# A mixer's numerator summed by an accumulating DMA instead of VectorE, in a two-layer recurrent mixer and mixture-of-experts kernel

## The reference

```python
ek = jnp.exp(jnp.minimum(kf, 30.0))
ekv = ek * vf
# forward and reverse scans over time, a = a * decay + ekv, b = b * decay + ek
euk = jnp.exp(jnp.minimum(u + kf, 30.0))
num = nf + nb - ekv + euk * vf
den = df + db - ek + euk
base = jax.nn.sigmoid(r) * (num / jnp.maximum(den, 1e-08))
out = base * (0.8 + 0.2 * tf)
```

## Time and profile before

| what | value |
|---|---|
| three runs, median (lowest to highest) | 4678.69 us (4672.37 to 4686.97) |
| the profiled execution's span | 4682.9 us |
| TensorE busy in it | 4475.7 us, 96% |
| VectorE busy in it | 2567.2 us, 55% |
| units alone | 0 to about 317 us |
| units beside halves 0 to 5 | about 317 to 1546 us |

### The profile page before, as it was taken

How to read it: one execution, slowest core, us unless ns; L and a number is a source line. 1 busy time by engine, 2 the same in 40 slices (tenths; PEclk the granted TensorE clock), 3 DMA queues, 4 the chain that set the end, 5 groups by cost and what they waited for, 6 DMA issues and landing times.

```text
span 4682.9 us, 60901 instructions
## 1 busy us (share of the span) xinstructions
PE 4475.7 (96%) x19862; PEld 3545.7 (76%) x19863; DVE 2567.2 (55%) x2765; ACT 1789.8 (38%) x2596; POOL 722.8 (15%) x934
## 2 busy tenths in 40 slices
PE   6777999999999999999999999999999999999998
PEld 2245877777777877878888888888888888888887
DVE  8999999999999653433233434444341253333432
ACT  5665555555555333232222323334231142222321
POOL 1000000000000017211111112112111121111111
PEclk8888999999999999999999999999999999999999
DMA  6675767767676766754344545555552254444543
GB/s 226 235 263 184 274 241 268 251 223 282 240 268 226 270 212 190 251 182 111 95 131 112 170 112 160 171 166 150 182 168 57 61 186 145 112 112 116 161 109 61
DMA packets 247928, 835.08 MB, mean 178 GB/s; under 512 B 28160, under 2 KB 61056, under 8 KB 222976
## 3 DMA queue, kind: packets, MB, share of 16 engines
q1 hardware_dynamic: 172944, 572.77, 34.5%
q0 software_dynamic: 47728, 160.07, 15.5%
q10 hardware_dynamic: 27136, 100.67, 5.8%
HBM read 652.40 MB, written 181.01 MB: 178 GB/s over the span
## 4 chain that ended last, share of the span: by engine, by line
PE 80%; DVE 10%; issue 4%; ACT 3%; DMA 2%; POOL 0%; ACTq 0%; DVEq 0%; POOLq 0%; SPq 0%
PE ps L1593 34%; PE ps L1457 22%; PE ps L1607 16%; PE ps L1526 3%; PE ps L1479 1%; PE ps L1582 1%; DVE work L969 1%; DVE work L975 1%; DMA work<-rows_dram,row_idx 1%; PE ps L1477 1%; PE ps L1467 1%; DVE work L996 1%; DVE work L998 1%; DVE work L972 1%; DVE work L1002 1%
## 5 line engine op out<-in xcount | busy, mean ns | idle before, releaser
L1593 PE MATMUL ps<-halves 128*128 128x512 f32 x7152 | 1698.6, 393 | 3.5 <-DVE halves L1356 2.8
L1593 PEld LDWEIGHTS ps<-halves 128*128 128x128 f32 x7152 | 1338.5, 189 | 279.9 <-DVE halves L1356 3.1
L1457 PE MATMUL ps<-halves 128*128 128x512 f32 x6144 | 1450.2, 395 | 13.7 <-issue 12.5
L1457 PEld LDWEIGHTS ps<-halves 128*128 128x128 f32 x6144 | 1154.1, 189 | 287.2 <-issue 47.8
L1607 PE MATMUL ps<-halves 128*128 128x512 f32 x3576 | 834.9, 389 | 1.3 <-DVE halves L1372 1.3
L1607 PEld LDWEIGHTS ps<-halves 128*128 128x128 f32 x3576 | 671.1, 188 | 140.9 <-DVE halves L1372 1.6
L1356 DVE TENSOR_TENSOR halves<-ps,halves 128x1024 fp32r<-128x1024 f32 x150 | 183.7, 1225 | 905.2 <-ACT halves L852 905.2
L1351 DVE TENSOR_TENSOR halves<-work,halves 128x1024 fp32r<-128x1024 f32 (+1 forms) x320 | 440.2, 1433 | 83.6 <-ACT halves L856 83.3
L852 ACT ACTIVATE halves<-ps 128x1024 fp32r<-128x1024 f32 x150 | 154.0, 1027 | 862.4 <-PE ps L1593 862.4
L576 POOL DMA_INDIRECT out<-work,add_idx x149 | 249.8, 1677 | 1417.3 <-DVE work L1378 1382.2
L856 ACT ACTIVATE halves<-work 128x1024 fp32r<-128x1024 f32 (+1 forms) x320 | 369.1, 1229 | 67.0 <-PE ps L1607 56.5
(11 more groups left out here) (186 smaller groups left out, 3674.4 us busy)
## 6 DMA issues: line engine op xcount, KB each, us to landing
halves<-split_dram SPq DMA_DIRECT2D x512, 512.0 KB, 5.6
work<-expert_w SPq DMA_DIRECT2D x192, 1024.0 KB, 5.5
split_dram<-halves ACTq DMA_DIRECT2D x32, 1024.0 KB, 4.9
plain<-shared_w SPq DMA_DIRECT2D x32, 512.0 KB, 3.2
gated_dram<-work ACTq DMA_DIRECT2D x32, 512.0 KB, 4.1
work<-side_t ACTq DMA_DIRECT2D x32, 512.0 KB, 5.6
work<-x_t ACTq DMA_DIRECT2D x32, 512.0 KB, 3.7
ratio_dram<-work ACTq DMA_DIRECT2D x32, 512.0 KB, 4.2
```

The source lines that it names most:

```text
L1457: last = pe.matmul(bank(k % 4), w, op[:, part], start=(c == 0 and w is w_hi and op is hi), stop=(c == CB - 1 and w is w_lo))
L1593: last = pe.matmul(ps_h[:, a * 512:a * 512 + 512], xp[:, xk * P:(xk + 1) * P], wp[:, rhs], start=(xk == 0 and xp is xhi and wp is whi[q]), ...
```

## The change

In the units beside the halves VectorE no longer adds `W` to `G`. GpSimd waits for `W` and for the backward scan, and issues a DMA that reads `W` and adds it to `G` within SBUF. VectorE waits for the DMA's semaphore `num_added` before the last product. In all units the Newton products now work in `F`, so `W` keeps its content, and the wait for `num_w` (or `num`) ahead of the first of them is gone.

```diff
+ALONE = 2 * UNITS_PER_HALF
...
+            def add_numerator(u, l):
+
+                n = u * 2 + l
+                pool.wait_ge(s["wv_done"], n + 1)
+                pool.wait_ge(s["nb"], n + 1)
+                pool.dma_start(G, W, accum_op=ALU.add).then_inc(s["num_added"], 16)
+
             clip(0, 0)
-            with pool.Fori(0, BLOCKS // 2) as v:
+            with pool.Fori(0, ALONE // 2) as v:
                 clip(2 * v + 1, 1)
                 clip(2 * v + 2, 0)
+            for u in range(ALONE, BLOCKS):
+                add_numerator(u, 0)
+                clip(u + 1, (u + 1) % 2)
+                add_numerator(u, 1)
...
                     fill(4 * l + 2)
-                    if not summed_by_pe:
-                        ve.wait_ge(s["nb"], n + 1)
-                        ve.wait_ge(s["wv_done"], n + 1)
-                        ve.tensor_tensor(G, G, W, ALU.add).then_inc(s["num"], 1)
                     fill(4 * l + 3)
-                    if summed_by_pe:
-                        ve.wait_ge(s["num_w"], n + 1)
-                    else:
-                        ve.wait_ge(s["num"], n + 2)
                     ve.wait_ge(s["g_inv"], n + 1)
                     ve.wait_ge(s["den"], n + 1)
-                    ve.scalar_tensor_tensor(W, F, low[:, at], N, ALU.add, ALU.mult).then_inc(s["newton1"], 1)
+                    ve.scalar_tensor_tensor(F, F, low[:, at], N, ALU.add, ALU.mult).then_inc(s["newton1"], 1)
                     ve.wait_ge(s["newton1"], n + 1)
-                    ve.scalar_tensor_tensor(W, W, 2.0, N, ALU.subtract, ALU.mult).then_inc(s["newton2"], 1)
+                    ve.scalar_tensor_tensor(F, F, 2.0, N, ALU.subtract, ALU.mult).then_inc(s["newton2"], 1)
                     ve.wait_ge(s["newton2"], n + 1)
                     if summed_by_pe:
                         ve.wait_ge(s["num"], n + 2)
-                    ve.scalar_tensor_tensor(N, NUM if summed_by_pe else G, neg_gain[:, ds(u, 1)], W, ALU.mult, ALU.mult)\
+                    else:
+                        ve.wait_ge(s["num_added"], 16 * (n - 2 * ALONE + 1))
+                    ve.scalar_tensor_tensor(N, NUM if summed_by_pe else G, neg_gain[:, ds(u, 1)], F, ALU.mult, ALU.mult)\
```

More of the change, by code:

```diff
@@ L205, in adaln_moe @@
             "k_in x_in ramp consts_in cond_in kc ek ekv euk h_fwd h_edge h_bwd h_all den g_ln g_inv nf n_edge nb "
-            "wv_done num num_w newton1 newton2 sig_steps sig_x gated gated_raw ratio ratio_out gated_out "
+            "wv_done num num_w num_added newton1 newton2 sig_steps sig_x gated gated_raw ratio ratio_out gated_out "
             "split_hi split_lo split_pe chunk product read_out c_hi c_lo sig1_steps sig1 c1 z sq z_hi z_lo res "
```

## The result

| | median | lowest to highest | runs |
|---|---|---|---|
| before | 4676.17 us | 4672.37 to 4686.97 | 4 |
| after | 4721.45 us | 4719.62 to 4725.09 | 4 |

The ratio is 1.0093 with a 95% interval of 1.0081 to 1.0105: the change makes the kernel slower by about 45 us. The forecast was 4676, with a range up to 4698.

What follows compares the result with a forecast made beforehand. VectorE's order of work bounds up to 404, TensorE afterwards. Terms -1.8 + 0.3 - 1 = -2.5 us take the profiled 4682.9 to 4680.4; that span being 4.2 above the median, the forecast is 4676 us, 8-in-10 range 4656 to 4698.

Steps and rivals of the forecast that it cites:

- I take 5.5 us from the scan's end: Beside the halves: the accumulating DMA lands 5.5 us after the backward scan ends, 5.3 plus 0.2 for two semaphores.
- some 2 us: After 404: VectorE waits some 2 us per half for the adds, while eight numerators save 9.8 us.
- After 404 ... TensorE does not notice, since it is its own bound: Later halves: VectorE's savings and waits leave TensorE unaffected; 1 us was put for what VectorE's lag may have cost.
- The pieces are loaded three products ahead ...: hidden.: Dense halves: piece loads start some 18 us ahead against 6.1 us to land, so added DMA traffic costs nothing.
- The share that I had estimated, 0.82: Later halves: DMA engines' busy share rises from 0.71 to 0.82 with 8 x 512 KB more per half.
- where I said 1.8: Units running alone, before 317: no longer waiting for TensorE's W products saves 1.8 us.
- The three sums before 404: First half, before 404: three removed VectorE sums of 1.22 us save 3.7 us on the path.
- said 4.0: Three places before 404: VectorE waits 1.2 + 1.0 + 1.8 = 4.0 us for the adds.
- The clips between the adds: GpSimd's queue: a clip's late side load could delay the second layer's add in few units; nothing was put for it.
- rival 3: GpSimd, while issuing adds, is held by VectorE: 5.5 us becomes 7.0, some 4681 us; chance 0.12, inside "same".
- Rival 2: Adds land late among piece loads, VectorE waits: +6 to +7 us per later half, +11 in the first, 4720 us; chance 0.16.
- Rival 1: Later halves: VectorE's lag does hold them, so removing its sums gains some 20 us, 4656 us; chance 0.12.

Runs made afterwards that it cites:

- the first two experiments: Kernel before with Newton's products in F, sum kept, then also without the sum beside the halves: five halves 1031.5 and 1033.9 us.
- l = 0: Changed kernel with the DMA for the first layer's numerators only, VectorE summing the second's: 4686.32 us, ratio 1.0017 to before.
- l = 1: Changed kernel with the DMA for the second layer's numerators only, VectorE summing the first's: 4716.46 us, ratio 1.0078 to before.
- Newton in F: Kernel before with only Newton's products moved to F, the sum kept on VectorE: 4679.45 us, ratio 1.000 to before.
- the unwaited adding DMAs: Kernel before with Newton's products in F, sums kept, plus 48 accumulating 512 KB DMAs into DRAM scratch that VectorE doesn't await: 4697.02 us, ratio 1.0033.
- the plain transfers: Kernel before with Newton's products in F, sums kept, plus plain 512 KB DMAs into DRAM scratch that VectorE doesn't await: 4684.99 us, ratio 1.0011.

## Why the prediction was wrong

**The landing.** "I take 5.5 us from the scan's end" was the first step that failed. From the scan's end to the last product the 48 places take 7.8 us in the median, from 5.3 to 11.0 (in 7 of them VectorE does not wait). In the places where no other transfer is in the way it is 6.1 us. For a later half I had put a wait of "some 2 us"; the five halves wait 73.9 us, some 15 each. A place with nothing in the way, on the timeline of after:

```profile
772.70 2.34 DVE L995 TENSOR_TENSOR_SCAN work<-decay,edge_in,work 128x1024 f32<-128x1024 f32 x1
...
775.59 0.90 POOL L603 DMA_DIRECT2D work<-work  x1 [6.26 <-DVE work L995]
...
781.12 1.28 DVE L1008 SCALAR_TENSOR_TENSOR work<-work,neg_gain 128x1024 f32<-128x1024 f32 x1 [1.13 <-DMA work<-work]
```

From the scan's end at 775.04 it is 0.55 us to the issue where I had put 0.2 for two semaphores, and the issue takes 0.90 us, not the 0.63 of L602. The crowded kind:

```profile
718.77 4.22 SPq L397 DMA_DIRECT2D halves<-split_dram  x5
719.93 2.34 DVE L995 TENSOR_TENSOR_SCAN work<-decay,edge_in,work 128x1024 f32<-128x1024 f32 x1
...
722.83 0.91 POOL L603 DMA_DIRECT2D work<-work  x1 [6.80 <-DVE work L995]
...
732.98 1.28 DVE L1008 SCALAR_TENSOR_TENSOR work<-work,neg_gain 128x1024 f32<-128x1024 f32 x1 [4.95 <-DMA work<-work]
```

The DMA engines in the 3 us after that issue, where none of the add's packets has started yet, and after the undelayed issue:

```profile
724.30:727.40 3.10, 3.09 (x14) 2.39 (x13) 3.06 (x4) 2.31 (x4) 0.00 (x0) 1.00 1.00 314
775.60:777.00 1.40, 1.40 (x8) 1.13 (x6) 1.40 (x4) 1.40 (x3) 0.90 (x1) 1.00 0.57 228
```

Just before the add SP had issued six piece loads (the view begins behind the issue of the first), and the engines are full with them (share 1.00). This add takes 10.7 us from the scan's end. Loads that are issued just behind the add delay it too. The add that lands 9.7 us after its issue, in the stretch at 531 to 544 shown above, had no transfer issued in the 5 us before it:

```profile
534.07 0.87 POOL L603 DMA_DIRECT2D work<-work  x1 [26.30 <-DVE work L995]
534.12 0.33 SPq L426 DMA_DIRECT2D work<-ratio_dram  x1
534.55 0.85 SPq L397 DMA_DIRECT2D halves<-split_dram  x2
```

An add's first packet starts 1.4 us after its issue at the earliest, and by then the packets of these three fill the engines (share 1.09 from 535.5 to 537.5). Five of the 48 adds are of this kind, with landings of 7.6 to 9.7 us. I had taken the scatter's median as the landing beside "other transfers", but a share of 0.71 as a mean over a half is made of stretches at 1.00 and at little, and the piece loads come in the former. The Trainium skill, page "DMA: Bandwidth & Descriptors", section "Anatomy of one DMA — SWDGE (gpsimd) path", gave an estimate of 3.2 us for 512 KB; the trace does not agree for an accumulating transfer, whose shortest landing is 4.6 us.

**VectorE's slack.** "After 404 ... TensorE does not notice, since it is its own bound" holds for a saving, and the comparison of the first two experiments shows it: 43 us less for VectorE change nothing. It does not hold for a wait. Savings of 1.22 us came spread over all places; waits come in a few, up to 5.3 us at once, and the steps of dense work queued behind them are late. The lag adds up: the timeline at 543.83 shows a stop of TensorE of 4.92 us after 14.0 us of waits in four places. The pair l = 0 and l = 1 prices it: 46 us of waits make 30 us of time. From Newton in F to the change, TensorE's stops over halves 1 to 7 rise from 35.7 to 61.1 us. Its clock takes a part as well. In the trace of after, TensorE runs at 1.2 GHz for some us at the end of each of its ten longest stops past 404 (3.0 to 12.2 us). By the records of the granted clock, what it loses at that level in halves 1 to 7 is 27 us after the change, 17 before, 10 with Newton in F. (It is an estimate: half of the time spent at the lower level.) With the traffic equal it is 15 us with l = 0 alone and 27 with l = 1 alone, so the waits seem to take part. But it is 22 us with the unwaited adding DMAs already, and before and Newton in F, which take the same time, differ by 7: how the clock's part divides between waits and traffic is not shown.

**"The pieces are loaded three products ahead ...: hidden."** Wrong, by about 17 us, as the unwaited DMAs show. The share that I had estimated, 0.82, was right in size (0.78), but it did not price the traffic. Accumulating costs more than the bytes: the plain transfers cost about 5.

**The sum of the loss.** From Newton in F (no difference from before) the traffic leads to 1.0033, about +17 us, and the rest up to 1.0093, about +28 us, comes with making VectorE wait. Both together are the 45 us. What stays open: the unwaited DMAs go from DRAM to DRAM, the ones of the change within SBUF, and how the 17 us divide between engine time and DRAM was not told apart. So the split is an estimate. That waits, with the traffic equal, cost what they do is shown by l = 0 against l = 1.

**What was right.** Newton's products in F save at the end of the units alone: the last product of unit 7 stands at 306.0 instead of 310.0, 4.0 us where I said 1.8. The three sums before 404 were worth 3.6 us (399.3 less 395.7; said 3.7). There the adds cost: VectorE waits for them 5.2 us (said 4.0), and with x and the ratios late too the first normalization is at 404.4, within a microsecond of before as forecast, though 5.1 us later than Newton in F alone has it. The clips between the adds cost nothing, and nothing shows rival 3: the issue takes 860 to 956 ns in all 48 places.

**The rivals.** Rival 2, to which I gave 0.16, named the mechanism and nearly the number, 4720. It said "It decides from about 7.8 us on", and 7.8 was the measured median. Its argument against, that nearly all landings lie close together, was the misreading: those of the earlier trace rows are from the expert stretch, where the page of before has the DMA engines busy 2 to 5 tenths in every slice. But it came to its sum partly by luck, since it let VectorE's total fill the half (209 us, and 214 with idle time), and work and waits come to some 203 (187.06, and a fifth or sixth of 88.6) in a half of 215; the traffic's 17 us were no part of it, and its +11 us in the first half did not come (404.4 against 403.9). Rival 1 is excluded: with the sums gone and nothing in their place the later halves are no shorter.

## What to carry to other kernels

Before work is moved from an engine with slack to a DMA, look at the moment of its issue, not at the mean share: which transfers are issued in the 5 us before it and the 1 us behind it, and is the cover longer than the landing beside them. An engine that is 95% busy beside another can be relieved of work without any gain, and still cost the kernel when it stands still, since the steps queued behind the wait feed the bound. The last microseconds of waiting are the dear ones: here a third to two thirds of each (16 us of time for 48 of waiting, 30 for 46), while the first 41 us of waits cost 3 to 8 us on top of the traffic. And 25 MB more of DMA traffic that nobody waits for are not free beside a stretch bound by TensorE: run them alone, with the work left in place, before the rest is built.

## What was not expected of the hardware

An accumulating DMA of 512 KB within SBUF lands in 4.6 us at the shortest and 7.1 in the median; the scratch transfers of that size from the same queue take 7.1 us accumulating and 4.9 plain beside the same work, and the packets of 4 KB take about twice as long on a DMA engine (0.33 against 0.16 us). The issue of the accumulating one holds GpSimd 0.90 us, against 0.63 for L602. And a TensorE that has stood still for 4.92 us, as before 547.03, goes on at half its clock: 10 products in 4 us, and 20 in the next 4.
